# Layer 1's attention in a two-layer decoder: a head's 128 dimensions in one chunk of partitions, scores as one matmul per head, rotation by shifted products

## What is computed

```python
q = h @ Wq.T                                   # 16 heads x 128
k = h @ Wk_down.T @ Wk_up.T + k_anchor         # 4 heads x 128, through a rank of 64
v = h @ Wv_down.T @ Wv_up.T + v_anchor
def rotate_half(x): x1, x2 = split(x, 2, axis=-1); return concatenate([-x2, x1], -1)
q = q * cos + rotate_half(q) * sin             # cos and sin repeat after 64 dimensions
k = k * cos + rotate_half(k) * sin
scores = einsum('bhqd,bhkd->bhqk', q, repeat(k, 4)) / sqrt(128)
attn = softmax(where(causal, scores, -1e9))
x = x + einsum('bhqk,bhkd->bhqd', attn, v) @ Wo.T
```

## Time and profile before

| | |
|---|---|
| median of 3 runs | 1869.06 us (1868.19 to 1871.84) |
| the profiled execution's own time | 1871.72 us |
| its span | 1869.9 us |
| TensorE busy | 1792.0 us, 96% |
| VectorE busy | 998.8 us, 53% |
| ScalarE busy | 606.0 us, 32% |
| GpSimd busy | 409.6 us, 22% |
| mean granted TensorE clock | 0.984 |

### The profile page before, as it was taken

The page is one execution under the profiler, slowest core; times in us unless marked ns, Lnnn a source line. Parts: engine busy times, 40 slices in busy tenths (PEclk is TensorE's granted clock), DMA queues, the critical chain, the costliest instruction groups (busy, mean ns, idle before and its releaser), DMA issues.

```text
span 1869.9 us, 29060 instructions
## 1 busy us (share of the span) xinstructions
PE 1792.0 (96%) x11730; PEld 1179.7 (63%) x11730; DVE 998.8 (53%) x1892; ACT 606.0 (32%) x1931; POOL 409.6 (22%) x488
## 2 busy tenths in 40 slices
PE   7999999999999999999889999998999999999998
PEld 6766666646665665666555888876577674444444
DVE  4765666426666666557644111116645455565887
ACT  1233222315555565555640111110312213232511
POOL 2432323512020220120003000006121020002476
PEclk9999999999999999999998999999999999999999
DMA  9100002000000000000214988965000021643011
GB/s 377 42 1 1 1 1 107 1 15 18 18 18 15 4 18 18 1 17 2 113 69 174 368 331 327 339 254 198 27 1 1 1 107 50 250 161 124 3 38 40
DMA packets 31109, 170.62 MB, mean 91 GB/s; under 512 B 3865, under 2 KB 3865, under 8 KB 17185
## 3 DMA queue, kind: packets, MB, share of 16 engines
q1 hardware_dynamic: 28416, 161.43, 22.9%
q0 software_dynamic: 2560, 7.34, 1.3%
HBM read 155.91 MB, written 16.52 MB: 92 GB/s over the span
## 4 chain that ended last, share of the span: by engine, by line
PE 83%; DVE 9%; POOL 4%; ACT 2%; issue 2%; DMA 1%; SPq 0%; POOLq 0%; DVEq 0%
PE PS L1142 8%; PE PS L985 6%; PE PS L1222 6%; PE PS L936 6%; PE PS L1019 5%; PE PS L1058 4%; PE PS L1010 4%; PE PS L1286 4%; PE PS L1182 4%; PE PS L1151 4%; PE PS L1255 3%; PE PS L1042 3%; PE PS L1273 3%; PE PS L1078 2%; PE PS L993 2%
## 5 line engine op out<-in xcount | busy, mean ns | idle before, releaser
L2046 POOL TENSOR_TENSOR rstd<-veps,mhalf 112x1 f32<-112x1 f32 (+1 forms) x76 | 58.0, 764 | 577.2 <-DVE veps L1315 554.0
L1142 PEld LDWEIGHTS PS<-R,W 128*128 128x128 f32 x1344 | 155.8, 195 | 11.8 <-issue 11.8
L1142 PE MATMUL PS<-R,W 128*128 128x128 f32 x1344 | 156.2, 278 | 2.2 <-DVE R L1610 2.2
L1439 DVE TENSOR_REDUCE nmx<-PS 112x2 f32<-112x750 f32 x128 | 114.0, 931 | 81.4 <-PE PS L1042 81.4
L1910 ACT ACTIVATE R<-PS,nmx 112x375 f32<-112x375 f32 x256 | 142.9, 573 | 3.7 <-DVE nmx L1439 3.7
L936 PE MATMUL PS<-xT,W 128*128 128x224 f32 x640 | 127.1, 359 | 1.1 <-DMA W<-in_w0kv 0.8
L936 PEld LDWEIGHTS PS<-xT,W 128*128 128x128 f32 x640 | 123.0, 194 | 7.7 <-issue 5.5
L1617 DVE TENSOR_TENSOR R<-R,PS 128x512 f32<-128x512 f32 x21 | 14.5, 688 | 201.7 <-PE PS L1142 201.7
L1387 DVE TENSOR_TENSOR x<-x,PS 112x512 f32<-112x512 f32 x40 | 27.5, 687 | 170.0 <-PE PS L985 82.4
L1255 PE MATMUL PS<-W 128*128 128x512 f32 x256 | 117.6, 602 | 0.0
L985 PE MATMUL PS<-W,R 128*112 128x512 f32 x256 | 113.7, 597 | 0.0
(11 more groups left out here) (291 smaller groups left out, 3233.7 us busy)
## 6 DMA issues: line engine op xcount, KB each, us to landing
W<-in_we SPq DMA_DIRECT2D x63, 1024.0 KB, 8.3
W<-in_entwT SPq DMA_DIRECT2D x8, 1024.0 KB, 7.3
W<-in_entpw SPq DMA_DIRECT2D x8, 1024.0 KB, 8.5
W<-in_ctxT SPq DMA_DIRECT2D x8, 750.0 KB, 4.2
R<-in_ctxT SPq DMA_DIRECT2D x8, 750.0 KB, 8.4
R<-in_ctx SPq DMA_DIRECT2D x8, 750.0 KB
xs_rows<-in_x SPq DMA_DIRECT2D x3, 1792.0 KB, 38.2
R<-xs_rows SPq DMA_DIRECT2D x21, 256.0 KB, 9.1
```

The source lines that it names most:

```text
L1142: o = e.matmul(PS[:, m, c * 128:(c + 1) * 128], gate_up(j % 3, k, off + c * 128), BT[:, j % 2, k, :], start=k == 0, stop=k == 3)
L1439: e.tensor_reduce(nmx[0:S, par, r:r + 2], PS[0:S, r:r + 2, 0:SC], AX.X, ALU.max, negate=True).then_inc(*up("cmax", (b, c, par, r)))
```

## The change

The host lays out the query weights, the key-up weights and the key anchor so that group r of a `ku` or `kq1` step is all 128 dimensions of head r. `s1` becomes one matmul with 128 rows per head, 8 in place of 16. The sine table gets a sign: plus in partitions 0 to 63, minus in 64 to 127.

The rotation on VectorE now takes all 128 partitions times cos, and the two partition halves times sin, each written to the other half. For queries the bias is gone, and each of these 3 instructions covers both heads (448 elements). For keys, with an anchor per head, there are 3 instructions of 224 elements per head, 6 in all. GpSimd adds the two results in one instruction of 448 elements, after all of `rope_in`. Layer 0's rotation (`kq0`) stays as it was.

```diff
-    add("l1sin", np.sin(ang))
+    add("l1sin", np.where(p < 64, 1.0, -1.0).astype(f)[:, None] * np.sin(ang))
...
                 for j in range(4):
                     w.wait_ge(*at("rope", ("ku", u, g)))
                     w.wait_ge(*at("rope", ("kq1", u, 4 * g + j)))
-                    for ab in range(2):
-                        for r in range(2):
-                            ro = slice(64 * r, 64 * r + 64)
-                            o = e.matmul(PS[0:S, m + r, bcol(j)], LQ[ro, z, 4 * g + j, ab, bcol(i)], LK[ro, z, g, ab, bcol(i)],
-                                         start=ab == 0, stop=ab == 1)
+                    for r in range(2):
+                        o = e.matmul(PS[0:S, m + r, bcol(j)], LQ[:, z, 4 * g + j, r, bcol(i)], LK[:, z, g, r, bcol(i)],
+                                     start=True, stop=True)
...
+            def rope_in1(k, u, c, m):
+
+                w.wait_ge(*at("proj", (k, u, c)))
+                if (k, u, c) in rope_before:
+                    w.wait_ge(*at("rope", rope_before[k, u, c]))
+                low, high = slice(0, 64), slice(64, 128)
+                if k == "ku":
+                    for r in range(2):
+                        ps, n = PS[:, m, r * UT:(r + 1) * UT], 2 * c + r
+                        e.scalar_tensor_tensor(two(T4b[:, r, :]), two(ps), CL("kanch")[:, n:n + 1], over(C("l1cos"), UB),
+                                               ALU.add, ALU.mult)
+                        for of, to in ((high, low), (low, high)):
+                            o = e.scalar_tensor_tensor(two(T4b[to, 2 + r, :]), two(ps[of]), CL("kanch")[of, n:n + 1],
+                                                       over(C("l1sin"), UB)[of], ALU.add, ALU.mult)
+                    o.then_inc(*up("rope_in", (k, u, c)))
+                    return
+                ps = PS[:, m, 0:2 * UT].rearrange("p (a n) -> p a n", n=S)
+                cos, turned = T4b[:, 0:2, :], T4b[:, 2:4, :]
+                four = [t.rearrange("p a n -> p (a n)").rearrange("p (a n) -> p a n", n=S) for t in (cos, turned)]
+                e.tensor_tensor(four[0], ps, over(C("l1cos"), 2 * UB), ALU.mult)
+                for of, to in ((high, low), (low, high)):
+                    o = e.tensor_tensor(four[1][to], ps[of], over(C("l1sin"), 2 * UB)[of], ALU.mult)
+                o.then_inc(*up("rope_in", (k, u, c)))
...
             def rope(k, u, c):
                 dst, _, _, _, T4 = rope_of((k, u, c))
+                if k != "kq0":
+                    w.wait_ge(*at("rope_in", (k, u, c)))
+                    e.tensor_tensor(dst, T4[:, 0:2, :], T4[:, 2:4, :], ALU.add).then_inc(*up("rope", (k, u, c)))
+                    return
...
-    q = kmaj(i["L1_attn_Wq"].T).reshape(128, 4, 2, 2, 4, 2, 64).transpose(0, 2, 4, 1, 5, 3, 6)
+    q = kmaj(i["L1_attn_Wq"].T).reshape(128, 4, 2, 2, 4, 2, 64).transpose(0, 2, 4, 1, 3, 5, 6)
...
-    ku = i["L1_attn_Wk_up"].reshape(2, 2, 2, 64, 64).transpose(4, 0, 2, 1, 3).reshape(64, 512)
+    ku = i["L1_attn_Wk_up"].T
...
-        i["L1_attn_k_anchor"].reshape(2, 2, 2, 64).transpose(1, 3, 0, 2).reshape(128, 4),
+        i["L1_attn_k_anchor"].reshape(4, 128).T,
```

More of the change, by code:

```diff
@@ L878, in rope_of @@
                 return Q[z][:, c], "q0cos", "q0sin", [bq[:, 2 * c + n:2 * c + n + 1] for n in range(2)], T4a
[L879 to L882, removed]
+            return (LK if k == "ku" else LQ)[:, z, c], "l1cos", "l1sin", None, T4b
         ropes = [s for s in order if s[0] in ("kq0", "ku", "kq1")]
@@ L1328, in rope_in @@
                 m = bank_of[k, u, c][0]
-                _, cos, sin, (ba, bb), T4 = rope_of((k, u, c))
+                _, cos, sin, bias, T4 = rope_of((k, u, c))
+                if k != "kq0":
+                    rope_in1(k, u, c, m)
+                    return
+                ba, bb = bias
                 A, B = two(PS[:, m, 0:UT]), two(PS[:, m, UT:2 * UT])
```

## The result

The kernel after the change takes 1882.47 us (1881.73 to 1883.86, 6 runs), the kernel before in the same comparison 1868.62 (1866.30 to 1871.84). The ratio is 1.0074, with a 95% interval of 1.0061 to 1.0087: slower by about 14 us. The forecast was 1871.0, with a range up to 1875.2.

A forecast was written before the change was run, and what follows sets the result against it. The chain was taken to run on TensorE for 83%, with VectorE binding unit 0's opening. Opening 4.4 plus rest 0.6 minus matmuls 3.0 gave +2.0 us on the median 1869.06: 1871.0, range 1866.8 to 1875.2.

The forecast's parts named there:

- VectorE's price of the products: Layer 1 rotations: a `kq1` needs 1.59 us, 0.40 more, a `ku` 2.16, 0.72 more; 18.6 us added in all.
- It just fits: Units 1 to 3: the VectorE and GpSimd loop takes 3.0 us per `kq1` against TensorE's 3.06.
- Costed at nothing: Units 1 to 3: late mask and value-product copy cost nothing; without the cover up to 1.5 us, three times.
- The opening, +4.4: Unit 0's opening: longer rotations among the `mix` steps delay norms, second `s1` mask and value product by 4.4 us.
- The 0.45 us of contention: Opening: GpSimd's sum beside a `mix` takes 0.45 us longer, added to the new sum's 1.14.
- the 2 to 6 that I gave: Sign of error: the value product of 1323.36 moving by under 2 or over 6 us; expected at about 1327.8.
- The matmuls: Score steps `s1`: 16 records take 1.57 us to the transpose, with no 0.10 in front; a step saves 0.34 us.
- The sum of 3.0: Score steps over the whole kernel: eight full savings of 0.34 us, plus 0.15 and 0.14, save 3.0 us.
- The rest: Units 1 and 3: the later second `ku` delays a `kq1` behind `vp1`, 0.4 us in unit 1, 0.2 in unit 3.
- The shared interface: Rival, opening: a sum beside a `mix` gets nothing until both `mix` instructions end; +2.7 us, 1873.7; chance 0.08.
- The clock: Rival: longer opening stalls prolong TensorE's low clock, losing up to 3.4 us, 1874.5; chance 0.20.
- Hidden, faster: Rival: opening hidden, sum 0.95 us, half-height products cheap, low clock falls into the stall; 1866.5; chance 0.12.

The follow-up runs named there:

- three_full: Kernel after the change, each half-height product replaced by a full-height one, uncrossed, the first to spare columns (another rotation computed); 1874.00 us, ratio 1.0019.
- before_two_buffers: Kernel before the change plus a second buffer for layer 1's four products, nothing of the change; 1865.64 us, ratio 0.9979.
- s1_only: Kernel before with only the scores changed to 8 matmuls of 128 rows, old rotation and layout (other scores computed); 1868.67 us, ratio 0.9994.
- s1_old_form: Kernel after the change with its scores as 16 matmuls of 64 rows again (other scores computed); 1881.86 us, ratio 1.0066.
- late_sum_only: Kernel before with only GpSimd's layer 1 part changed: one 448-element sum after all four products (another rotation computed); 1871.85 us, ratio 1.0011.
- two_full: Kernel after the change with each pair of half-height products made one full-height product, uncrossed (another rotation computed); 1868.40 us, ratio 0.9997.

## Why the prediction was wrong

**The failed step is VectorE's price of the products**, with the "It just fits" that hung on it. "A `kq1` needs 3 x 0.53 = 1.59 us" took the spacing of full-height products for the halves. I saw that no row had 64 partitions or crossed halves, and allowed a tenth more. Measured: 0.64 for the first and 1.29 for the two halves to the next instruction's start, 1.93, a fifth more. A `ku` was priced at 6 x 0.36 = 2.16 and takes 2.80 (1283.88 to 1286.68), 0.46 to 0.47 each. three_full has the spacings of the forecast, and 1874.0 us, inside the range. The 8.5 us between it and the change are this step, out of the 11.5 by which the forecast was too low. The other 3.0 are three_full's distance from the forecast; in its trace the opening has 1.8 of them.

**"It just fits"** fell with it. The loop went from 3.0 to 3.21 against TensorE's 3.06. I had looked at a longer sum as the danger (1.36), not at longer products; the sum took 1.13 to 1.15, as forecast. "Costed at nothing" became the 1.86 us wait and the low clock in unit 3.

**The opening, +4.4** (three_full: +6.2, after: +9.6). From `kq1` 0 to 1, the forecast took the longer of two ways: VectorE's own, 1.59 + 1.8, and the one over the sum, 3.5. The 0.45 us of contention were put on GpSimd's sum only. They fall on both: the sum beside the `mix` lasts 1.57 in three_full (in the kernel after 1.70 or, where it isn't slowed, 1.13), and the `mix` pair 2.28 or more in place of 1.84. VectorE's own way was 1.59 + 2.21 = 3.8 there, and 1.93 + 2.22 = 4.15 after. With four such places and the four-instruction `mix` (3.28 to 3.96), the lag relative to the start of the opening (1274.0 before, 1272.6 after) grows to 1.3 us at `kq1` 0 (forecast 0.7), 2.5 at 1 (1.2), 5.4 at 4, and 9.0 at `kq1` 7. The value product of 1323.36 waits for a copy of VectorE that ends at 1331.51 in place of 1323.20. It comes over 8 us later, outside the 2 to 6 that I gave.

**The matmuls.** The local price was right: 1.57 us, no 0.10 in front. The sum of 3.0 isn't shown. From the end of the opening to the last `w1`, three_full needs 266.7 us, the kernel before 269.7, which is 3.0; but 1.2 of it lie in the first piece (29.6 against 30.8), and before_two_buffers, with the old matmuls, has 29.6 there too. s1_only's trace has 1.9 up to unit 3 and 0.7 with the tail, mostly because of its clock. No median shows the saving: s1_only is 0.6 us faster than the kernel before, the change 0.6 us slower than s1_old_form, and both are within the noise.

**The rest.** The `kq1` block behind `vp1` waits 0.55 us (forecast 0.4). Not foreseen: the longer `ku` rotation holds its bank, and an output product waits 0.3 to 0.4 us for it, three times.

**The rivals.** The shared interface was real in another form: no sum waited for both `mix` instructions, but each engine made the other longer, and late_sum_only puts it at 2.6 us. That this is near the 2.7 of that rival is luck, for the way there is another. The clock is not the main cause. The mean granted clock of the opening is 0.96 before, 0.89 after and 0.85 in three_full. At two levels, full and half, that is an estimate of 4, 13 and 17 us at the low one. Yet three_full's opening is 3.4 us shorter than that of the kernel after, and VectorE's own times account for the pitch. What part of the opening's last microseconds is the clock's wasn't separated. "Hidden, faster" is refuted.

## What to carry to other kernels

In these runs a product of 64 partitions costs VectorE as much as one of 128 (0.62 us for 448 elements), and more if it starts in other partitions than its neighbour: splitting by halves to shift data across partitions doubles the instructions and ends their overlap. Before halving work on an engine that is not the bottleneck, work out its loop with the spacing that the new shape will have, compare it with the bottleneck's pitch, and leave room: 3.0 against 3.06 was none. Where a cheaper matmul is bought with more elementwise work, first take away the handover between the elementwise engines; here that buffer alone gave 3.8 us, more than the change did even with its halves for nothing (two_full).

## What the runs showed that was not expected

- A held start costs 0.10 to 0.11 us an instruction (0.63 to 0.64 against 0.53 to 0.54 for 448 elements, 0.46 to 0.47 against 0.36 for 224). A different start partition on one side, input or output, is enough for it.
- A GpSimd sum and VectorE's `mix` make each other longer, and which one pays more depends on how they meet. The pair lasts 1.52 us with no sum beside it, 1.84 beside a sum of 224 elements, 2.28 beside one of 448. In the kernel after (VectorE's `mix` at 1289.90 is shown above):

```profile
1289.95 1.70 POOL L2091 TENSOR_TENSOR R<-R 128x448 f32<-128x448 f32 x1 [2.08 <-DVE R L1362]
...
1302.59 2.51 DVE L1649 SCALAR_TENSOR_TENSOR x<-R,x 112x512 f32<-112x512 f32 x2
...
1302.64 1.13 POOL L2091 TENSOR_TENSOR R<-R 128x448 f32<-128x448 f32 x1 [2.54 <-DVE R L1362]
```

  At 1289.90 both pay: the sum takes 1.70 us in place of 1.13, and of the two `mix` instructions the first lasts 0.75 as ever and the second 1.50. At 1302.59 the sum isn't slowed at all, and the pair pays 0.99 us. It looks as if the two engines took turns by whole instructions; no run tests that.
- The scaling L1680 at 1322.63 lasts 1.89 us beside a sum in the kernel after.
- Full-height score matmuls with half the instructions saved 1.9 us of TensorE's trace up to unit 3, and 0.6 us of 1869 in the median, which the noise covers. A saving on the engine that holds 83% of the chain is worth what the next wait and the granted clock leave of it.
